# Projection matmuls of a mixed-weights LoRA layer: mixes cut in three, weight rows re-spaced, product order turned

## What is computed

```python
# x: (64, 64, 1024); condition: (64,) in 0..15; cond weights: (16, 64, 64)
W = weights[condition]
y = einsum('bct,bcd->bdt', x, W)                  # the "mix": one 64x64 matrix per sample
gate_logits = einsum('bsd,ed->bse', y, gate_w)    # 8 experts
w, sel = top_k(gate_logits, 2); w = softmax(w)
w_full = sum(one_hot(sel, 8) * w[..., None], axis=2)
result = einsum('bsd,od->bso', y, base_w) + base_b
low = einsum('bsd,erd->ebsr', y, lora_A)          # 8 experts x rank 16 = 128 columns
result += 2.0 * einsum('ebsr,eor,bse->bso', low, lora_B, w_full)
out = x + result
```

## Time and profile before

| | |
|---|---|
| median of three runs | 494.07 us |
| the profiled execution, whole | 493.61 us |
| its span, first to last instruction | 491.5 us |
| outside the span | 2.1 us |
| PE busy / PEld busy | 487.4 / 479.2 us, 2771 instructions each |
| DVE / ACT / POOL busy | 370.8 / 382.3 / 129.5 us |
| granted clock of PE | full in all 40 slices (2.4 GHz) |

### The profile page before, as it was taken

How to read it: one execution, slowest core, us unless ns; L and a number is a source line. 1 busy time by engine, 2 the same in 40 slices (tenths; PEclk the granted TensorE clock), 3 DMA queues, 4 the chain that set the end, 5 groups by cost and what they waited for, 6 DMA issues and landing times.

```text
span 491.5 us, 8738 instructions
## 1 busy us (share of the span) xinstructions
PE 487.4 (99%) x2771; PEld 479.2 (97%) x2771; DVE 370.8 (75%) x801; ACT 382.3 (78%) x740; POOL 129.5 (26%) x111
## 2 busy tenths in 40 slices
PE   9999999999999999999999999999999999999997
PEld 8999999999999999999999999999999999999996
DVE  4977878778787778787777777787877787777654
ACT  4888778878778887778887788787788877887620
POOL 2033302333203333123332223332133320233121
PEclk9999999999999999999999999999999999999999
DMA  8812122121222231221221222212212212211112
GB/s 333 353 43 98 50 91 95 56 98 62 84 91 73 76 96 52 92 91 53 96 73 72 89 85 65 96 53 91 91 53 96 92 55 88 96 53 55 55 44 85
DMA packets 31986, 43.89 MB, mean 89 GB/s; under 512 B 18402, under 2 KB 22370, under 8 KB 31970
## 3 DMA queue, kind: packets, MB, share of 16 engines
q1 hardware_dynamic: 31826, 43.17, 25.1%
q10 hardware_dynamic: 144, 0.52, 0.4%
HBM read 25.00 MB, written 18.68 MB: 89 GB/s over the span
## 4 chain that ended last, share of the span: by engine, by line
PE 97%; ACT 2%; DVE 0%; issue 0%; POOL 0%; ACTq 0%; POOLq 0%
PE acc L654 80%; PE acc L687 9%; PE mixed L674 6%; ACT y_moved L366 1%; PE acc L783 1%; PE mixed L660 1%; ACT x_parts L353 0%; ACT w_raw L358 0%; DVE w_raw L470 0%; DVE y_turned L477 0%; ACT y_hi L389 0%; DVE w_raw L556 0%; ACT lowT_hi L381 0%; POOL zeros L273 0%; PE acc L681 0%
## 5 line engine op out<-in xcount | busy, mean ns | idle before, releaser
L654 PE MATMUL acc<-w_hi,y_hi 128*128 128x384 f32 (+3 forms) x768 | 257.3, 338 | 0.0
L654 PE MATMUL acc<-w_lo,y_hi 128*128 128x384 f32 (+3 forms) x768 | 257.0, 338 | 0.0
L654 PE MATMUL acc<-w_hi,y_lo 128*128 128x384 f32 (+3 forms) x768 | 256.7, 338 | 0.0
L366 ACT COPY y_moved<-w_raw 32x256 f32<-32x256 f32 x480 | 194.1, 404 | 37.8 <-DVE w_raw L470 32.1
L298 POOL TENSOR_TENSOR w_raw<-x_sb,bias 128x1024 f32<-128x1024 f32 x32 | 77.2, 2413 | 344.1 <-DVE low L525 258.4
L654 PEld LDWEIGHTS acc<-w_hi,y_hi 128*128 128x128 f32 x768 | 144.0, 188 | 3.8 <-ACT w_hi L339 0.2
L654 PEld LDWEIGHTS acc<-w_lo,y_hi 128*128 128x128 f32 x768 | 143.9, 188 | 2.8
L654 PEld LDWEIGHTS acc<-w_hi,y_lo 128*128 128x128 f32 x768 | 143.9, 188 | 0.6 <-DVE y_lo L455 0.3
L470 DVE TENSOR_TENSOR w_raw<-mixed,w_raw 64x1024 f32<-64x1024 f32 x60 | 73.0, 1217 | 30.2 <-ACT w_raw L358 29.8
L477 DVE STREAM_TRANSPOSE y_turned<-y_moved 128x512 f32<-128x512 f32 x60 | 42.3, 706 | 51.4 <-ACT y_moved L366 51.4
L358 ACT COPY w_raw<-mixed 64x1024 f32<-64x1024 f32 x60 | 60.9, 1015 | 21.4 <-PE mixed L674 20.6
(11 more groups left out here) (56 smaller groups left out, 238.9 us busy)
## 6 DMA issues: line engine op xcount, KB each, us to landing
x_sb<-in_x SPq DMA_DIRECT2D x32, 512.0 KB, 3.3
out<-w_raw SPq DMA_DIRECT2D x31, 512.0 KB, 2.6
w_raw<-in_proj_w SPq DMA_DIRECT2D x8, 580.0 KB, 9.5
scratch<-low_squares SPq DMA_DIRECT2D x29, 64.0 KB, 1.5
lowT_raw<-scratch SPq DMA_DIRECT2D x116, 16.0 KB, 1.7
cw<-in_cond_w ACTq DMA_DIRECT2D x1, 512.0 KB, 3.6
lb_raw<-in_lora_b SPq DMA_DIRECT2D x1, 512.0 KB, 16.3
bias<-in_base_b SPq DMA_DIRECT2D x1, 512.0 KB, 17.1
```

The costliest lines, as they stand in the source:

```text
L366: done = nc.scalar.copy(y_moved[q * SQ:(q + 1) * SQ, g, :, :], piece.rearrange("m (k q a) -> m q k a", q=QUARTERS, a=SQ)[:, q, :, :])
L654: return nc.tensor.matmul(acc[:, c % 2, b, 0:hi - lo], y_part[:, c % 2, k, :], w_part[:, k, lo:hi], start=(k == 0 and product == 0), stop= ...
```

## The change

Three edits, all to what PE reads and in which order. Every mix goes as matmuls of 512, 256 and 256 columns where it went as two of 512. The split weights get rows of 1216 columns (4864 bytes = 19 x 256) and begin 48 columns (192 bytes) into a row, so every row of every bank begins 192 bytes past y's blocks, modulo 256. And in steps 1 to 30 the nine matmuls of a k go product by product, three banks each; the wait for `res_ready` goes along with the first matmul into bank 2, which is now the third of the step and was the seventh. Step 0 and step 31 keep their order.

```diff
+    PITCH, FIRST = 1216, 48
...
-        w_hi = sb("w_hi", [P, KT, N], F32R)
-        w_lo = sb("w_lo", [P, KT, N], F32R)
+        w_hi_rows = sb("w_hi_rows", [P, KT, PITCH], F32R)
+        w_lo_rows = sb("w_lo_rows", [P, KT, PITCH], F32R)
+        w_hi = w_hi_rows[:, :, FIRST:FIRST + N]
+        w_lo = w_lo_rows[:, :, FIRST:FIRST + N]
...
-                for h in range(2):
-                    last = nc.tensor.matmul(mixed[:, h, :], w_sel[:, c % 2, b, :],
-                                            x_parts[:, c % 2, b, h * 512:(h + 1) * 512], start=True, stop=True)
+
+                for lo, hi in ((0, 512), (512, 768), (768, 1024)):
+                    last = nc.tensor.matmul(mixed[:, lo // 512, lo % 512:lo % 512 + hi - lo], w_sel[:, c % 2, b, :],
+                                            x_parts[:, c % 2, b, lo:hi], start=True, stop=True)
...
-                    for b in range(3):
-                        if k == 0 and b == 2 and c >= 2:
-                            pe.wait_ge(res_ready, s - 1)
-                        for product in range(3):
+                    for product in range(3):
+                        for b in range(3):
+                            if k == 0 and product == 0 and b == 2 and c >= 2:
+                                pe.wait_ge(res_ready, s - 1)
                             done = project(c, k, b, product)
```

## The result

The changed kernel takes 496.74 us (496.22 to 497.18, five runs) against 493.85 us (493.81 to 494.27, five runs) of the kernel before: ratio 1.0055, 95% interval 1.0044 to 1.0067. It is slower by 2.9 us. The forecast was 492.6 us, faster, with a range of 490.6 to 495.3 us; the result lies above it.

The account below looks back on a forecast made before the run. PE alone bounds the kernel, by matmul count times start-to-start distance. From the profiled 493.61 us, +0.2 (mixes), -1.56 (layout), -0.1 (step 31) give 492.15; with 0.46 to the median 492.6 us, 8-in-10 range 490.6 to 495.3.

Parts of the forecast that it names:

- What bounds the kernel: PE is busy 99% of the span and nearly nothing waits; time is matmul count times start-to-start distance.
- the layout's term: Projection matmuls, all rows at offset 192: 1.576 us for nine, 6.5 ns less than average, 240 blocks, -1.56 us.
- the plain pace: Projection pace from the line through experts and mixes: 1.570 us for nine matmuls; -3.0 us if all blocks go at it.
- the first sign of being wrong: Prediction wrong if the nine projection matmuls still differ between the k: then the offset isn't what sets them.
- The order: Product by product in the steps: between nothing and +2.3 us, below nothing as well; taken as nothing beyond the layout's middle.
- that rival: Slower, the order sets the pace: step 0's 1.592 us in 240 blocks, +2.3 us, 496.6 us; chance 0.19.
- It would be a coincidence if it hit the average of eight different ones: Argument against the "nothing that counts changes" rival (493.1 to 495.0 us, chance 0.31): one offset makes every k's pattern the same.
- The mixes: 60 mix calls, each with one matmul more, 463.4 ns where two of 512 took 460: +0.2 us.
- The wait for res_ready, and the cover of y: At a step's third matmul, DVE L556 ends 0.87 us earlier; y's second half is split 1.7 us before k = 0.
- The loads: PEld counts as many as PE, 2831 both; the rival that the edit saves loads: under 2 in 100, 491.1 us at best.
- Step 31: Its 24 matmuls of 256 columns at offset 192: some 3 ns each, and a little on other banks, -0.1 us.
- The rule: PE's two independent SBUF read ports: neither offset nor order changes anything, only the mixes' +0.2 us left; called second rival.

Follow-up runs that it names:

- layout_only: The kernel before with only the weight rows' offset of 192 bytes in all rows (bank by bank order, mixes of 2 x 512): 494.90 us, ratio 1.0018.
- order_only: The kernel before with only the product order (offsets 32 k, mixes of 2 x 512): 495.21 us, ratio 1.0024.
- mix_only: The kernel before with only the mixes cut into 512, 256 and 256: 494.08 us, ratio 1.0004.
- no_cut: The changed kernel with the mixes as before, 2 x 512 (product order and offset 192 stay): 496.56 us, ratio 1.0052.
- cut_head: The changed kernel with mixes of 256, 256 and 512 columns, the 512 last: 490.59 us, ratio 0.9930 to the kernel before.

## Why the prediction was wrong

**What bounds the kernel** was right: PE alone, start to start, no waits. The move is all there, and in PE's distance, as the whole of it had been counted (240 blocks of nine).

**The failed step** is in the layout's term: "So I take the offset to be worth up to 30 ns in nine matmuls", and from it the value of 1.576 us for offset 192, the middle between the plain pace, to which step 31 pointed, and k = 6 of the steps. With it the layout stood in the sum at -1.56 us; alone, it measured +0.94 (layout_only). The pace isn't a property of the offset alone, and the first sign of being wrong came true: the nine still differ between the k. At offset 192 and in the product order, nine matmuls took 1.560 us (k = 7), 1.58 (k = 1) and 1.600 (k = 2 to 6) in one and the same kernel, by what ran before them. Both rows were read rightly where they stood; but there the neighbours had other offsets, and neither could say what 192 does when all rows have it. The blocks of nine came to 12.74 / 8 = 1.5925 us on average in place of 1.576: 240 x 16.5 ns = 4.0 us, which is nearly the whole error of 4.1 us. In the range I had put the end at 1.60 for every block (+4.2 us), but gave it little weight, and so the range ended at 495.3.

**The order.** I took nothing for it, for want of a row, and kept +2.3 us as a rival, by step 0's 1.592 us. Zero was the wrong value: alone, the order costs +1.25 us (order_only). The time came out at that rival's 496.6 us almost to the point, but not as it said, with one pace of the order in all blocks. Step 0 of the changed kernel, the same product order at offset 192, is at 0.52 us for three from 13.27 on, 0.03 us less for nine than before. Only the layout differs there, so the slow pace of step 0 was a matter of it, as the text had against this rival. That the number was met is luck; a rival isn't shown by that.

**"It would be a coincidence if it hit the average of eight different ones"** pointed at the right thing, that one common offset makes all k alike, and drew too little from it: a pattern that repeats exactly can also repeat its worst case, so the two ends of this term deserved more weight than the middle.

**The mixes.** The term was +0.2 us; alone, it measured +0.12 (mix_only), within the interval of nothing. In the changed kernel the cut costs more itself (0.46 and 0.47 us where no_cut has 0.45 twice) and gives it back in k = 0 and 1. Small in both, but not additive: the same cut turned around (cut_head) is worth 6.1 us there. I had priced the mixes by their columns alone, and never asked what follows them.

**The wait for res_ready, and the cover of y.** Right: PE has the same two waits as before (1.1 and 0.2 us), neither of them at this matmul, and DVE L560 ends at 203.61 + 0.41 = 204.02, before the step's first matmul at 204.56.

```profile
203.61 0.41 DVE L560 TENSOR_TENSOR w_raw<-acc,w_raw 128x256 f32<-128x256 f32 x1
```

**The loads.** Right: 2831 of both. **Step 31**: the bank of 256 columns did go faster, as offset 192 had let expect: k = 2 to 7 take 2.05 us after (below), and took 488.12 - 486.00 = 2.12 before, about the 0.1 us of the sum.

```profile
488.77 0.28 PE L658 MATMUL acc<-w_hi_rows,y_hi 128*128 128x256 f32 x1
...
490.82 0.28 PE L692 MATMUL acc<-lb_hi,lowT_hi 128*128 128x256 f32 x1
```

**The rule.** By the Trainium skill (SBUF — State Buffer, "Who interferes with whom") the two read ports of PE are independent; from this the prediction had drawn that layout and order would do nothing. The runs don't agree: layout_only alone moved the time by 0.18% (1.0009 to 1.0027) and cut_head against the changed kernel by over 1%, with the same counts of everything; whatever the cause is, layout and order do set the pace of the matmuls of this kernel.

## What to carry to other kernels

When PE is the bound and never waits, read starts to starts in groups that repeat, and see at which instruction the pace changes: here it changed at a mix or at the experts, and a reordering of three small matmuls decided over 1.2% of the time. A pace that was read amid other neighbours can't be taken over to a layout in which everything is alike; the alike case is new, and wants a measurement of its own. And before giving up a change that came out slower, vary what stands between its repeating parts: the order and the offset of this change, each slower alone, are both needed for the fastest kernel found here, cut_head at 490.59 us, and the cut is needed the other way round (four pieces did as well, 490.77 us).

## What the runs showed of the hardware that was not expected

- Three projection matmuls (384, 384 and 392 columns) settle on 0.520, 0.527 or 0.533 us in the product order, with one offset of 0 or 192 bytes, and stay there over 12 groups of three in a row and more (21 in step 0 of the changed kernel), at the full clock. The steps between are 6.7 ns, which is 16 cycles at 2.4 GHz. At 32 bytes they take 0.53 and 0.52 us in turn.
- A short different sequence moves the pace. At offset 192: 512 + 256 + 256 columns by one step slower, 2 x 512 from 0.520 to 0.533 (to 0.527 with x at another address), 256 + 256 + 512 and 4 x 256 not beyond the first three matmuls, the nine matmuls of the experts back from 0.533 to 0.520.
- The fastest pace that was kept, 0.520 us for 1160 columns, is 0.448 ns a column with the fixed parts in it; the line through experts and mixes has 0.443 without them. No run kept a faster one.
